# Score maxima inside the next expert tile, narrow value products and on-chip values in a four-stage kernel with attention

## The reference

```
x = x + diffusion(x)                        # second differences in both directions, and a logistic term
x = x + sum_e gate_e * (silu(x Wg_e) * (x Wu_e)) Wd_e      # 8 experts and a shared one, hidden width 512
x = x + lora(x, language)                   # rank 16, one of 4 per block
x = x + attention(seq1 = x, seq2 = side)    # 16 heads of 8, masked keys, each query also sees itself
```

## Time and profile before

| | |
|---|---|
| median of three runs | 522.89 us |
| profiled execution | 520.16 us |
| its span | 518.4 us |
| TensorE busy | 464.0 us, 90% |
| VectorE busy | 338.3 us, 65% |
| ScalarE busy | 273.6 us, 53% |
| GpSimd busy | 179.8 us, 35% |
| DMA moved | 37.29 MB |

### The profile page before, as it was taken

The page is one execution under the profiler, slowest core; times in us unless marked ns, Lnnn a source line. Parts: engine busy times, 40 slices in busy tenths (PEclk is TensorE's granted clock), DMA queues, the critical chain, the costliest instruction groups (busy, mean ns, idle before and its releaser), DMA issues.

```text
span 518.4 us, 7084 instructions
## 1 busy us (share of the span) xinstructions
PE 464.0 (90%) x1894; PEld 341.5 (66%) x1894; DVE 338.3 (65%) x682; ACT 273.6 (53%) x592; POOL 179.8 (35%) x187
## 2 busy tenths in 40 slices
PE   5886795959699999999999999999998877999995
PEld 2665674738587888887888887888873534555542
DVE  4485594756466766666666667766865764888853
ACT  2564372726345555655556554555554543666663
POOL 3558283744322213221313231354751111222220
PEclk8799797988889999999999999999998997999998
DMA  5324143341200120000020000022226345555600
GB/s 166 102 82 139 53 121 115 79 138 28 76 9 0 28 77 3 0 1 0 21 82 0 0 0 0 18 87 64 62 73 180 76 120 165 162 166 163 177 23 21
DMA packets 44921, 37.29 MB, mean 72 GB/s; under 512 B 4408, under 2 KB 39388, under 8 KB 44892
## 3 DMA queue, kind: packets, MB, share of 16 engines
q1 hardware_dynamic: 43440, 36.64, 24.5%
q0 software_dynamic: 1024, 0.26, 0.3%
q10 hardware_dynamic: 432, 0.10, 0.1%
HBM read 26.07 MB, written 10.66 MB: 71 GB/s over the span
## 4 chain that ended last, share of the span: by engine, by line
PE 71%; issue 8%; DMA 6%; DVE 6%; SPq 5%; ACT 2%; POOL 2%; ACTq 0%; DVEq 0%; POOLq 0%
PE pv_ps L695 9%; PE g_ps L521 6%; PE g_ps L522 6%; PE acc_ps L521 6%; PE g_ps L523 6%; PE u_ps L521 5%; PE u_ps L522 5%; PE acc_ps L523 5%; PE acc_ps L522 5%; PE u_ps L523 5%; SPq L430 3%; PE st_ps L684 2%; DMA v_d<-stage 2%; PE s_ps L590 2%; DMA squares<-in_squares 1%
## 5 line engine op out<-in xcount | busy, mean ns | idle before, releaser
L802 ACT ACTIVATE act_p<-g_ps 128x512 f32<-128x512 f32 x144 | 86.2, 599 | 157.0 <-PE g_ps L523 156.7
L1053 DVE TENSOR_TENSOR u_ps<-act_p,u_ps 128x512 f32<-128x512 f32 x144 | 100.0, 695 | 88.3 <-PE u_ps L523 83.7
L1257 POOL TENSOR_TENSOR xg_lo<-xg,xg_hi 128x512 fp32r<-128x512 f32 x35 | 45.6, 1304 | 165.2 <-ACT xg_hi L812 165.1
L1057 DVE TENSOR_TENSOR act_lo<-u_ps,act_hi 128x512 fp32r<-128x512 f32 x144 | 98.3, 683 | 0.1
L807 ACT ACTIVATE act_hi<-u_ps 128x512 fp32r<-128x512 f32 x144 | 85.5, 594 | 3.2 <-DVE u_ps L1053 3.2
L695 PE MATMUL pv_ps<-probs_t,v_blocks 128*128 128x512 f32 x128 | 68.5, 617 | 3.7 <-ACT v_blocks L895 1.9
L521 PE MATMUL acc_ps<-act_hi,w_split 128*128 128x512 f32 x144 | 59.4, 413 | 3.8 <-DVE act_lo L1057 3.8
L521 PE MATMUL g_ps<-x_hi,w_split 128*128 128x512 f32 (+1 forms) x144 | 59.2, 411 | 1.4 <-DVE x_lo L1082 1.4
L887 ACT ACTIVATE probs_t<-st_ps 128x512 f32<-128x512 f32 x64 | 37.9, 594 | 41.7 <-PE st_ps L684 41.4
L522 PE MATMUL g_ps<-x_lo,w_split 128*128 128x512 f32 (+1 forms) x144 | 57.9, 402 | 0.0
L523 PE MATMUL g_ps<-x_hi,w_split 128*128 128x512 f32 (+1 forms) x144 | 57.6, 400 | 0.0
(11 more groups left out here) (147 smaller groups left out, 745.5 us busy)
## 6 DMA issues: line engine op xcount, KB each, us to landing
k_blocks<-k_rows SPq DMA_DIRECT2D x32, 96.0 KB
q_plain<-q_rows SPq DMA_DIRECT2D x8, 384.0 KB
q_blocks<-q_rows SPq DMA_DIRECT2D x32, 96.0 KB
k_plain<-k_rows SPq DMA_DIRECT2D x8, 384.0 KB
v_both<-v_d SPq DMA_DIRECT2D x8, 272.0 KB, 3.0
w_raw<-in_L_cond_Wg SPq DMA_DIRECT2D x8, 256.0 KB, 2.9
w_raw<-in_L_cond_Wu SPq DMA_DIRECT2D x8, 256.0 KB, 3.0
w_raw<-in_L_cond_Wd SPq DMA_DIRECT2D x8, 256.0 KB, 3.0
```

Of the source, the lines that this page charges most:

```text
L802: activation(act_p[k % 3][:], g_ps[k % 3][:], ACT.Silu).then_inc(silu_done, 1)
L1053: tt(u_ps[k % 3][:], act_p[k % 3][:], u_ps[k % 3][:], ALU.mult).then_inc(prod_done, 1)
L1057: tt(act_lo[k % 3][:], u_ps[k % 3][:], act_hi[k % 3][:].bitcast(F32), ALU.subtract).then_inc(act_lo_done, 1)
L1257: tt(xg_lo[e % 3][:], xg[:].rearrange("p b s -> p (b s)"), xg_hi[e % 3][:].bitcast(F32), ALU.subtract)\
```

## The change

All 144 slots and 64 groups of attention are written out, without hardware loops.

**Steps.** Each tile t does its own `side` (slot 16), `query` (18) and `natural` (20, 22, 24, 26), and `diffuse` of tile t+1 (slot 14). `bias` is at slot 6, `setup` at 9. The five finishing steps of a tile are at slots 3, 5, 8, 10, 12 of the next.

**Maxima.** Scores and maxima of tile t-1's blocks are made in slots 17 to 32 of tile t, one group per slot, in one bank; keys for them are loaded per block into `k_blk` and `q_pl` (6 DMAs). The maxima of a block are turned at slots 23, 27, 31, 35, stored to DRAM and loaded with the pair. Those of tile 3 are made in blocks 4 to 11 of the attention.

**Values.** `v_all`, `v_self` and `x3_all` hold all blocks on chip; 12 blocks are loaded at the end of the experts, the last four are written directly. A value product has nine columns of weights and 128 columns of one head.

**Buffers.** Gate banks, `xg_hi` and `xg_lo` go from three to two, `x1` from four to two; the pair buffers go from two to three.

```diff
+FINISH_SLOT = {3: "lora_a", 5: "lora_b", 8: "key", 10: "value", 12: "x_natural"}
+SETUP_SLOT = {6: "bias", 9: "setup"}
+DIFFUSE_SLOT, SIDE_SLOT, QUERY_SLOT, NATURAL_SLOT = 14, 16, 18, 20
+SCORE_SLOT, TURN_AFTER = 17, 6
...
+            def load_keys(b):
+                n, tok = b % 2, slice(b * S, b * S + S)
+                sp.wait_ge(rows_stored, rows_count("key", b // TB))
...
+                for j in range(GJ):
+                    r = slice(3 * DH * j, 3 * DH * (j + 1))
+                    sp.dma_start(k_blk[n][r, :, j].bitcast(F32), k_rows[r, :, tok]).then_inc(keys_loaded[n], 16)
...
+            for t in range(NT):
+                for k in range(SLOTS):
...
+                    for kind, f, b in before_slot(t, k, 2):
+                        stores_of(kind, f, b)
+                        if kind == "diffuse" and f + 1 < NT:
+                            load_x(f + 1)
+                        if kind == "key":
+                            load_keys(f * TB)
+                            load_keys(f * TB + 1)
+                    if k == DIFFUSE_SLOT - 3:
+                        load_side(t)
...
+            sp.wait_ge(down_done, SLOTS * (NT - 1) + FC * VALUES_AFTER)
+            sp.wait_ge(v_stored, 16 * (NT - 1))
+            sp.dma_start(v_all[:, 0:done].rearrange("p b h w -> p b (h w)"), blockwise(v_prev_d[0:done])).then_inc(values_loaded, 16)
...
+            sp.dma_start(v_self[:].rearrange("p b h r -> p b (h r)"), blockwise(v_self_d)).then_inc(values_loaded, 16)
...
+            stores_of("key", NT - 1, 0)
+            load_keys(done)
+            load_pair(3)
+            load_keys(done + 1)
+            store_out(0)
+            load_pair(4)
...
+                    turned = turn_at(t, k)
+                    if turned is not None:
...
+                        turn_max(turned, b * GI + i + 1, s_ps)
+                    up_product(t, k)
+                    for step in steps_at(t, k):
...
+                        aux_step(*step)
+                    if t * SLOTS + k >= LAG:
+                        down_product(t * SLOTS + k - LAG)
+                    scored = score_at(t, k)
+                    if scored is not None:
+                        scores(*scored, s_ps)
...
-                mm(pv_ps[i // 2][:], v_blocks[n % 2][:, window:window + 128], probs_t[i][:].rearrange("p j s -> p (j s)"),
-                   start=(i % 2 == 0), stop=(i % 2 == 1)).then_inc(pv_written, 1)
+                for j in range(GJ):
+                    last = mm(pv_ps[b % 2][COLS * j:COLS * j + VW, i * S:(i + 1) * S], v_all[:, b, i * GJ + j],
+                              probs_t[m % 3][:, j], start=True, stop=True)
+                last.then_inc(pv_written, 1)
...
+            pe.wait_ge(pv_cleared, 2)
+            pe.wait_ge(values_loaded, 32)
...
+            def take(b):
+                dve.wait_ge(pv_written, b * GI + GI)
+                wait(dve, pv_turned, b - 1)
+                nc.vector.tensor_copy(pv_own[b % 2][:].rearrange("p i s -> p (i s)"), pv_ps[b % 2][:]).then_inc(pv_taken, 1)
```

More of the change, by code:

```diff
@@ L37 @@
 VW = DH + 1
-HALVES = 2
-VROW = 32 // HALVES
-V_STEP = 128 + VROW
+COLS = 32
 PAIR = 2
 NP = B // PAIR
[L52 to L59, removed]
+PBUF = 3
 WARM_PRODUCTS = 4
-MIX_AHEAD, SQUARE_AHEAD = 6, 4
 AHEAD = 3
-LAST_AUX = {(0, 1): 0, (0, 2): 1, (1, 1): 2, (1, 2): 3, (1, 3): 4}
@@ L65 @@
[L65 to L75, removed]
+LAG = 2
+FINISH = ["lora_a", "lora_b", "key", "value", "x_natural"]
+FINISH_SLOT = {3: "lora_a", 5: "lora_b", 8: "key", 10: "value", 12: "x_natural"}
+SETUP_SLOT = {6: "bias", 9: "setup"}
@@ new lines, with steps_at @@
+DIFFUSE_SLOT, SIDE_SLOT, QUERY_SLOT, NATURAL_SLOT = 14, 16, 18, 20
+SCORE_SLOT, TURN_AFTER = 17, 6
+LATE_FINISH = {(0, 0): "lora_a", (0, 2): "lora_b", (1, 0): "key", (1, 2): "value", (2, 0): "x_natural"}
+LATE_SCORES = {(4 + n * 2 + i // 2, i % 2 * 2 + 1): (B - TB + n, i) for n in range(TB) for i in range(GI)}
+LATE_TURN = {(6 + n * 2, 0): B - TB + n for n in range(TB)}
+def steps_at(t, k):
+    out = []
+    if t == 0 and k in SETUP_SLOT:
+        out.append((SETUP_SLOT[k], 0, 0))
+    if t > 0 and k in FINISH_SLOT:
+        out.append((FINISH_SLOT[k], t - 1, 0))
+    if k == DIFFUSE_SLOT and t + 1 < NT:
+        out.append(("diffuse", t + 1, 0))
+    if k == SIDE_SLOT:
+        out.append(("side", t, 0))
+    if k == QUERY_SLOT:
+        out.append(("query", t, 0))
+    if k >= NATURAL_SLOT and (k - NATURAL_SLOT) % 2 == 0 and (k - NATURAL_SLOT) // 2 < TB:
+        out.append(("natural", t, (k - NATURAL_SLOT) // 2))
+    return out
@@ new lines, with before_slot, after_slot @@
+ORDER = [("diffuse", 0, 0)] + [s for t in range(NT) for k in range(SLOTS) for s in steps_at(t, k)]
+ORDER += [(kind, NT - 1, 0) for kind in FINISH]
+NTH = {step: n for n, step in enumerate(ORDER)}
+ROUNDED = [s for s in ORDER if s[0] in ("diffuse", "side", "query", "lora_b", "key")]
+NTH_ROUNDED = {step: n for n, step in enumerate(ROUNDED)}
+def before_slot(t, k, by):
+    t, k = (t, k - by) if k >= by else (t - 1, k - by + SLOTS)
+    return steps_at(t, k) if t >= 0 else []
+def after_slot(t, k, by):
+    t, k = (t, k + by) if k + by < SLOTS else (t + 1, k + by - SLOTS)
+    return steps_at(t, k) if t < NT else []
@@ L182, in build @@
[L182 to L202, removed]
@@ L577, in later_step, with scores @@
                 else:
[L578 to L579 removed]
+                    for c in range(TB):
+                        last = turn(aux_ps[:, c * S:(c + 1) * S], x3_t[:, c], ident)
                 last.then_inc(aux_written, 1)
[L582 to L585 removed]
+            def scores(b, i, bank):
                 if i == 0:
[L588 to L591 removed]
```

1220 lines of the change are left out of this document (557 added, 663 removed).

## The result

The changed kernel takes **526.7 us** (median of 20 runs, 520.4 to 534.1) against 521.1 us before (20 runs, 516.6 to 523.5). The ratio is **1.007**, interval 1.004 to 1.011. The ratios leave out runs in which the chip granted a lower clock, which is why this one lies under the quotient of the medians; the traces of two experiments (SP's order, all edits together) are of such runs, and in them waits are read for their place and not for their exact size. The forecast was 500 us, 474 to 526, and faster by over 1%. It was wrong: the kernel did not get faster, and its span is 22.5 us over the sum. The profiled run is 521.2 us with a span of 519.2; before it was 518.4.

The account below looks back on a forecast made before the run. TensorE was taken to bound all but tile 0 and the attention's front. Terms -46.6 + 23.9 + 6 + 26.6 - 31.6 = -21.7 turned 518.4 into 496.7, 498.5 with 1.8 outside; forecast 500 us, range 474 to 526.

Parts of the forecast that it names:

- Tile 0: First tile: keeps one tile's steps instead of four, takes 87 us instead of 133.6, a gain of 46.6.
- The new side wait: Tiles 1 to 3: TensorE waits for the side input behind key-row store and key loads; with low clock, +26.6 us.
- the rival of the worse queue: Slots 20 to 26: key loads and natural stores queue behind query rows, 8 us per tile, 524 us; chance 0.13.
- Work moved into tiles 1 to 3: Tiles 1 to 3: steps, scores and turns moved in add 23.9 us, plus 6 for waits at the turns.
- Value products: Attention: a group of four narrow products on four strips takes 0.53 us, a block 4.1 instead of 6.30.
- five pass times: Value products: two passes follow each other per strip, the next strip starts beside the second; five times 0.107 us.
- serial: Rival, attention: strips follow each other, 0.86 us a group, a block 5.4, total 515.5 us; chance 0.22.
- exposed-load rivals: Rival, value products: narrow weight loads not hidden, +49 us on the serial case, total 564 us; chance 0.09.
- The clock in the attention: Start of the attention: a wait of 7.3 us for values, plus 1.6 us for the lower clock behind it.
- Queue waits: Attention: SP's queue lengthens 74.8 us to 80, keys of block 12 late for block 4, 14 late for block 8.
- a landing of 10.5 us: SP's row stores: 768 KB at 100 GB/s take 7.9 us, with issue and landing through 10.5 us after starting.

Follow-up runs that it names:

- SP's order: Changed kernel with SP's attention queue reordered (pair 3 before block 12's keys, block 14's keys before pair 5) and TensorE first waiting for v_all alone: 516.3 us, ratio 0.993.
- all edits together: Changed kernel with side input ahead of the key rows' store, SP's attention queue reordered, and row stores in 12 DMAs: 485.3 us, ratio 0.931 to the kernel before.
- the mended store in the kernel before: Kernel before the change with each row store cut into 12 DMAs of 32 partitions, nothing else: 490.9 us, ratio 0.947; run again 490.7 us, 0.943.
- the kernel with the keys first: Changed kernel with side input first, SP's attention queue reordered and stores in 12 pieces, but block 12's keys loaded before pair 3: 484.3 us, ratio 0.930.
- the experiment with one strip: Changed kernel with the four narrow value products of a group all writing the same strip of columns, only the time read: 544.3 us, one run.
- the kernel with both waits filled: Changed kernel with 24 overwritten score products before the wait for the values and 18 before block 12's scores: 528.6 us, ratio 1.010.
- the one with the wait for the values filled as well: Changed kernel with three edits, block 12's keys before pair 3, plus 14 overwritten score products before the wait for the values: 484.2 us, ratio 0.933.

## Why the prediction was wrong, step by step

- **Tile 0** was right: 87.5 us against 87, with no 6 us wait before a natural step. Inside it some terms offset each other: the natural step that was given 1 us of waiting stood 0.3, and the slot with the diffuse step took 3.0 over the pace against 1.7. That the old waits came from the row store is shown by the mended store in the kernel before.
- **The new side wait** was right in place, cause and size: 6.8, 7.1 and 9.4 us against 6.7, 6.7 and 8.4, behind 11.3 us of row store and two key loads. (Read with both of its terms, 1.2 of issue and 3.5 to land, the forecast's own sum would give 1.2 us more each time.) With the clock behind it, slots 16 and 17 took 8.0, 8.7 and 12.2 us more than in the kernel with the keys first: 28.9 against 26.6. The 2.3 over are tile 3's, where the half clock lasted 5.4 us instead of 3 and the wait was 1 us longer.
- **A wait at slot 25** stood in no term of the sum: the first scores of a tile's third block took 0.7 us more in tile 1 and 1.9 in tile 3. The profile names no releaser, but their key load is issued right behind the query rows' store, and the wait is gone wherever that store goes out in 12 pieces. It is the rival of the worse queue, at 2.5 us in all and not 24.
- **Work moved into tiles 1 to 3** was mis-sized. The kernel with the keys first, which has none of these waits, takes 92.4, 92.5 and 92.2 us there. In the last of them the turn at slot 27 stands 3.3 us where it stands 0.7 in the changed kernel; without that difference it is 89.6. The forecast had 89.8, 89.8 and 88.0 with the turns: 6.9 us too little. The turns' waits are 2.1 us in tile 1 where 2.0 stood. A slot with the diffuse step is 4.5 us, 2.5 over the slot pace where 1.7 stood, since 0.4 us of waiting and the first matmul's latency belong to it; the slot with the side input is 0.9 over, where 0.45 stood. The rest is spread over steps of 0.1 to 0.3 each and was not tried apart. These three items (2.3, 2.5 and 6.9) are the 11.6 us of the table, but for rounding.
- **Value products** went better than the term: 0.34 to 0.41 us a group against 0.53, so a late block takes 3.87 us against 4.1, 3.7 us less over 16. The picture behind 0.53, five pass times one after another, is not what the rows show. The serial and the exposed-load rivals are refuted by the experiment with one strip.
- **The clock in the attention** is the step that failed most. "A wait of 7.3, and 1.6 for the clock" took the price from a wait in tile 0, where full-width products follow, and gave the waits for keys no clock at all. (The sum also slips there: 11.5 less 4.6 is 6.9, nearer to the measured 6.7.) In the attention the half clock lasted 13 us behind the first wait and 19 behind the second. The blocks came out 9.8 us over the forecast: -3.7 for the faster groups, +5.2 for four turns that wait for `neg_split` on GpSimd (4.2 together) and one wait for ScalarE (1.0), which I had not seen, and 8.3 us that remain. That these are the half clock's is an estimate from what is left over. The 32 us at half clock are long enough for that, but the kernel with both waits filled had both stretches at full clock and was no faster. How the 8.3 us divide between the clock and SP's queue stays open.
- **Queue waits** of the attention were 5.4 us against the 5.2 in "80 (74.8)", but at block 12 and not shared with block 14.
- **What ties them together**: in the changed kernel's attention a gain in one place turned up as a loss in another. With the waits filled the lost time was a later wait for keys, which points to SP's queue as the pace; with the keys first it was a stretch at low clock with TensorE busy, which doesn't. In all, 42 products put into waits, 64 added, and 5 us of wait removed moved the time by 0.3, 0.8 and 0.15%.
- **The error of weighing**: the forecast counted a landing of 10.5 us as given and asked only where it would stand. The row with 95 to 105 GB/s beside 300 in the same line was itself a lever, worth 3% to the changed kernel, about as much as moving the side input, and 5% to the one before, the most that a single edit brought.

What stays open is why, beside narrow products on four strips, the clock falls or stays down in some stretches and not in others. The kernel with the keys first was at half clock from 448 to 458 us and at 1.00 after it; the one with the wait for the values filled as well was at 0.96 and then at 0.50, in the same blocks. Neither had a wait over 1.2 us in the 10 us before its low stretch.

## What to carry to other kernels

When a transfer runs at a third of the rate that the same line reaches later, look at the shape of its DMAs before moving work around its landing; cutting three stores into twelve took 5.3% off the kernel before, and the whole redesign nothing. A wait on TensorE has to be priced with the clock behind it, read from a stretch with the same kind of products: here, among narrow products on column strips, it was 13 and 19 us at half clock, and among full ones 3 to 5. And where an in-order queue sets the pace, look first at what stands in it: products put into TensorE's waits, and products added, changed the time by less than 1%, while two moves in the queue gave 3.4 and 1.5%.

## What the runs showed of the hardware that was not expected

Four 128x9 products on four strips take 0.41 us as a group and 1.04 on one strip, in fp32 with two passes each. A stretch of 8.8 us behind a wait of 5.2, with TensorE busy 8.79 of it, ran at a granted clock of 0.50; another of 10 us, busy throughout, ran at 0.53 with no wait over 1.2 us in the 10 us before it. Twelve DMAs of 64 KB went out at 117 to 156 GB/s where three of 256 KB went at 100, although SP spent 5.4 us instead of 1.7 on issuing them.
